# A curvature stage on five engines: one square per derivative, an identity product, and new orders

## The reference

```
g2 = ux * ux + uy * uy
denK = jnp.maximum(1.0 + g2, EPS)
K = jnp.clip((uxx * uyy - uxy * uxy) / (denK * denK + EPS), -5.0, 5.0)
denH = jnp.sqrt(1.0 + g2 + EPS)
H = ((1.0 + uy * uy) * uxx - 2.0 * ux * uy * uxy + (1.0 + ux * ux) * uyy) / (2.0 * denH ** 3 + EPS)
H = jnp.clip(H, -5.0, 5.0)
diff = jnp.clip(alpha * K + beta * H, -1.0, 1.0)
u = u + DT * diff
u = jnp.pad(u[:, :, 1:-1, 1:-1], ((0, 0), (0, 0), (1, 1), (1, 1)), mode='edge')
```

## Time and profile before

| | us |
|---|---|
| three runs | 699.22, 699.38, 702.49 (median 699.38) |
| profiled execution | 700.35 |
| its span | 698.5 |
| TensorE busy | 624.1 (89%) |
| VectorE busy | 389.5 (56%) |
| ScalarE busy | 314.6 (45%) |
| GpSimd busy | 253.5 (36%) |

### The profile page before, as it was taken

One profiled execution on the slowest core, in us unless ns is written; L12 is line 12 of the kernel. 1 busy time (PEld: TensorE's weight loads), 2 busy tenths in 40 slices (PEclk: granted clock), 3 DMA queues, 4 the chain that ended last, 5 costly groups with the idle time before them and its releaser, 6 DMA issues.

```text
span 698.5 us, 22687 instructions
## 1 busy us (share of the span) xinstructions
PE 624.1 (89%) x10128; PEld 362.1 (52%) x10128; DVE 389.5 (56%) x627; ACT 314.6 (45%) x582; POOL 253.5 (36%) x254
## 2 busy tenths in 40 slices
PE   5999699999996467778699879999999999999996
PEld 3785486466443233545355546555555555555551
DVE  4840000059213612223234427999999999999994
ACT  1300010043000001101122236999999999999993
POOL 1000000010001400000000006899999999999993
PEclk9999899999999766899999999999999999999999
DMA  9999999999999999999999544455455455455431
GB/s 367 433 420 381 426 432 425 427 429 421 430 424 422 431 426 428 428 429 424 429 424 423 187 120 128 116 132 136 126 132 135 128 131 136 127 131 138 125 84 61
DMA packets 33967, 201.69 MB, mean 289 GB/s; under 512 B 5504, under 2 KB 6928, under 8 KB 23632
## 3 DMA queue, kind: packets, MB, share of 16 engines
q1 hardware_dynamic: 33088, 198.53, 74.7%
q10 hardware_dynamic: 672, 1.41, 0.5%
q0 software_dynamic: 112, 0.32, 0.1%
HBM read 164.98 MB, written 1.84 MB: 239 GB/s over the span
## 4 chain that ended last, share of the span: by engine, by line
DVE 36%; PE 31%; DMA 26%; ACT 3%; issue 3%; SPq 0%; DVEq 0%; POOLq 0%; POOL 0%; ACTq 0%
DMA ring<-wout_w 16%; PE bank L407 8%; PE bank L423 7%; DVE ring L932 6%; DVE ring L935 6%; DVE ring L930 6%; PE bank L531 4%; PE bank L476 4%; DVE ring L928 4%; DMA ring<-wqk_p 3%; DVE ring L937 3%; DMA ring<-wv_w 3%; DMA ring<-wout_p 3%; DVE ring L956 3%; PE bank L557 3%
## 5 line engine op out<-in xcount | busy, mean ns | idle before, releaser
L597 PE MATMUL bank<-ring 32*32 32x480 f32 x5440 | 264.7, 570 | 2.6 <-DMA ring<-reg_a 2.6
L605 PE MATMUL bank<-ring 32*32 32x480 f32 x1600 | 177.3, 566 | 0.6 <-POOL ring L1148 0.6
L597 PEld LDWEIGHTS bank<-ring 32*32 32x32 f32 x5440 | 135.8, 103 | 70.9 <-issue 56.1
L1143 POOL TENSOR_TENSOR ring<-ring 128x480 f32<-128x480 f32 x40 | 48.9, 1223 | 178.5 <-DVE ring L935 178.5
L423 PE MATMUL bank<-ring,small 128*32 128x256 f32 x1152 | 81.6, 433 | 29.5 <-DMA ring<-wout_w 23.7
L423 PE MATMUL bank<-ring,xw 128*32 128x256 f32 x1024 | 61.8, 400 | 13.9 <-DMA ring<-wv_w 13.9
L423 PEld LDWEIGHTS bank<-ring,small 128*32 128x32 f32 x1152 | 40.0, 122 | 62.3 <-issue 30.0
L605 PEld LDWEIGHTS bank<-ring 32*32 32x32 f32 x1600 | 42.3, 104 | 56.9 <-issue 21.9
L407 PE MATMUL bank<-reg_a,ring 128*128 128x256 f32 x256 | 57.9, 388 | 3.4 <-DMA ring<-wqk_p 2.6
L767 DVE SCALAR_TENSOR_TENSOR reg_a<-bank,prm 128x512 f32<-128x512 f32 x4 | 2.8, 691 | 101.6 <-PE bank L483 101.6
L407 PEld LDWEIGHTS bank<-reg_a,ring 128*128 128x128 f32 x256 | 49.5, 195 | 11.6 <-DMA ring<-wqk_p 3.2
(11 more groups left out here) (181 smaller groups left out, 882.8 us busy)
## 6 DMA issues: line engine op xcount, KB each, us to landing
ring<-wv_w SPq DMA_DIRECT2D x32, 2048.0 KB, 28.4
ring<-wout_w SPq DMA_DIRECT2D x30, 2048.0 KB, 36.7
ring<-reg_a SPq DMA_DIRECT2D x60, 204.0 KB, 3.2
ring<-wqk_p SPq DMA_DIRECT2D x4, 2048.0 KB, 18.8
ring<-wqk_w SPq DMA_DIRECT2D x4, 2048.0 KB, 19.0
ring<-reg_a SPq DMA_DIRECT2D x60, 136.0 KB, 2.4
ring<-wv_p SPq DMA_DIRECT2D x2, 2048.0 KB, 18.9
ring<-wout_p SPq DMA_DIRECT2D x2, 2048.0 KB, 21.7
```

Source lines behind the costliest of these rows:

```text
L597: last = te.matmul(bank[QUAD * j:QUAD * (j + 1), field, 0:NF], mat(m, (j + t) % NCH), whole[at_, 2 + off:S + off, :], start=(n == 0), stop ...
L605: last = te.matmul(bank[at_, to, 0:NF], mat(m, j), from_[at_, :], start=start, stop=stop, skip_group_check=True)
L1143: p.tensor_tensor(cxy[now.q], f01[now.q][:, 0:NF], f01[now.q][:, NF:2 * NF], ALU.mult).then_inc(po["cxy"], 1)
```

## The change

Each first derivative is squared once. ScalarE squares uy into `p2`, as before, and ux straight into its bank (`sqr_x`); the bank's uy square is no longer ScalarE's work: TensorE multiplies `p2` by the identity into the bank of uy (`copy`), and outer waits for that. The arithmetic is otherwise the same.

All four engines get new orders inside the slot step, and some work changes its slot. In a step of TensorE, UYY and UXX are now those of now instead of old, the rest of UXY is that of old, and the first outer product is added at the end of the step for old. In a step of VectorE, clip2 and clip1 of now come first; then khk (old), the update and the edge copy (older), slope (now), khh (old), clipxy (now) and outer (now). ScalarE's new order is low (older), inverse of the first denominator (old), high (older), p2 and the x square (now), inverse of the second (old), the slope's logarithm, its square and its power 1.5, the square of uxy and the logarithm of both denominators (now). GpSimd's is the numerator of K (old), uxx·uyy and ux·uy (now), the two clips (old), cross (now). SP's program is not changed. A shortened diff:

```diff
 # TensorE
                 if old.live:
-                    te.wait_ge(ld_turn[2][old.c], 32 * (old.i + 1))
-                    if old.k > 1:
-                        te.wait_ge(ve["clip2"], old.k - 1)
-                    stencil(OUTER + 1, old, 3, UYY, 0)
-                    stencil(MIXED, old, 2, UXY, 2)
-                    ...
-                    stencil(OUTER, old, 1, UXX, 0)
-                    stencil(MIXED, old, 2, UXY, 3).then_inc(pe["fldxy"], 1)
-                if older.live:
-                    te.wait_ge(ve["outer"], older.k)
-                    add(bank_set(older.q) + 1, ONE, ab[older.q][:, 0:NF], True, False)
-                ...
+                    stencil(MIXED, old, 2, UXY, 1)
+                if now.live:
+                    te.wait_ge(ld_turn[2][now.c], 32 * (now.i + 1))
+                    if now.k > 1:
+                        te.wait_ge(ve["clip2"], now.k - 1)
+                    stencil(OUTER + 1, now, 3, UYY, 0)
                 if older.live:
                     add(bank_set(older.q) + 1, ONE, ab[older.q][:, NF:2 * NF], False, False)
+                if now.live:
+                    te.wait_ge(ld_turn[0][now.c], 32 * (now.i + 1))
+                    if now.k > 1:
+                        te.wait_ge(ve["clip2"], now.k - 1)
+                    stencil(OUTER, now, 1, UXX, 0)
                 if old.live:
+                    stencil(MIXED, old, 2, UXY, 2)
+                if now.live:
+                    stencil(OUTER + 1, now, 3, UYY, 1)
                 if older.live:
                     te.wait_ge(po["cross"], older.k)
                     add(bank_set(older.q) + 1, MINUS_TWO, cross[older.q], False, True).then_inc(pe["hn"], 1)
+                if now.live:
+                    stencil(OUTER, now, 1, UXX, 1)
                 if old.live:
+                    stencil(MIXED, old, 2, UXY, 3).then_inc(pe["fldxy"], 1)
+                if now.live:
+                    stencil(OUTER + 1, now, 3, UYY, 2)
+                    stencil(OUTER, now, 1, UXX, 2)
                 if old.live:
+                    te.wait_ge(ac["p2"], old.k)
+                    add(bank_set(old.q), ONE, p2[old.q], True, True).then_inc(pe["copy"], 1)
+                if now.live:
+                    stencil(OUTER + 1, now, 3, UYY, 3)
                     if now.k > 2:
                         te.wait_ge(ve["khk"], now.k - 2)
                     stencil(bank_set(now.q), now, 1, UY, 0)
+                    stencil(OUTER + 1, now, 3, UYY, 4).then_inc(pe["fld2"], 1)
+                    te.wait_ge(ld_turn[1][now.c], 32 * (now.i + 1))
+                    ...
+                    stencil(bank_set(now.q) + 1, now, 2, UX, 0)
                 ...
                     add(STEP, ALPHA, clip_k[older.q], True, False)
                 if now.live:
                     stencil(bank_set(now.q), now, 1, UY, 1)
                 ...
                     stencil(bank_set(now.q) + 1, now, 2, UX, 1)
                     stencil(bank_set(now.q), now, 1, UY, 2).then_inc(pe["fld1"], 1)
+                    if now.k > 1:
+                        te.wait_ge(ve["clipxy"], now.k - 1)
+                    stencil(MIXED, now, 2, UXY, 0)
+                if old.live:
+                    te.wait_ge(ve["outer"], old.k)
+                    add(bank_set(old.q) + 1, ONE, ab[old.q][:, 0:NF], True, False)
 # VectorE
+                if now.live:
+                    v.wait_ge(pe["fld2"], now.k)
+                    v.tensor_scalar(two(f34[now.q]), bank[:, OUTER:OUTER + 2, 0:NF], 10.0, -10.0, ALU.min, ALU.max).then_inc(ve["clip2"], 1)
                     v.wait_ge(pe["fld1"], now.k)
                     v.tensor_scalar(two(f01[now.q]), pair(now.q), 10.0, -10.0, ALU.min, ALU.max).then_inc(ve["clip1"], 1)
+                if old.live:
+                    ...
+                    v.tensor_tensor(kh[old.q][:, 0:NF], num[old.q], pair(old.q)[:, 0, :], ALU.mult).then_inc(ve["khk"], 1)
                 if older.live:
                     ...
+                if now.live:
+                    v.wait_ge(ac["p2"], now.k)
+                    v.wait_ge(ac["sqr_x"], now.k)
+                    v.scalar_tensor_tensor(slope[now.q], pair(now.q)[:, 1, :], 1.0, p2[now.q], ALU.add, ALU.add).then_inc(ve["slope"], 1)
                 if old.live:
                     ...
                     v.tensor_tensor(kh[old.q][:, NF:2 * NF], pair(old.q)[:, 1, :], inv_h[old.q], ALU.mult).then_inc(ve["khh"], 1)
+                if now.live:
+                    v.wait_ge(pe["fldxy"], now.k)
+                    v.tensor_scalar(mix[now.q], bank[:, MIXED, 0:NF], 10.0, -10.0, ALU.min, ALU.max).then_inc(ve["clipxy"], 1)
+                    v.wait_ge(ve["clip2"], now.k)
+                    v.wait_ge(pe["copy"], now.k)
+                    v.scalar_tensor_tensor(two(ab[now.q]), pair(now.q), 1.0, two(f34[now.q]), ALU.add, ALU.mult).then_inc(ve["outer"], 1)
# ScalarE
-                    a.activation(pair(old.q), f01[old.q].rearrange("p (x n) -> p x n", x=2), ACT.Square).then_inc(ac["sqr"], 1)
+                    a.activation(pair(now.q)[:, 1, :], f01[now.q][:, NF:2 * NF], ACT.Square).then_inc(ac["sqr_x"], 1)
```

More of the change, by code:

```diff
@@ L215, in build @@
             "slot_used", "patch_mean", "patch_var", "win_mean", "pool", "win_var", "pl_mean", "pl_var", "qkv",
-            "scores", "vt", "pt", "attn", "out", "ds", "conv", "fld1", "fld2", "fldxy", "step", "hn", "edge", "chunk")}
+            "scores", "vt", "pt", "attn", "out", "ds", "conv", "fld1", "fld2", "fldxy", "step", "hn", "edge", "chunk", "copy")}
         ve = {n: sem("ve_" + n) for n in (
@@ L655, in slot_step @@
                 if now.live:
[L656 to L660, removed]
                     stencil(bank_set(now.q), now, 1, UY, 1)
@@ L924, in slot_step @@
                 two = lambda a_: a_.rearrange("p (x n) -> p x n", x=2)
[L925 to L932, removed]
                 if now.live:
+                    v.wait_ge(pe["fld2"], now.k)
+                    v.tensor_scalar(two(f34[now.q]), bank[:, OUTER:OUTER + 2, 0:NF], 10.0, -10.0, ALU.min, ALU.max).then_inc(ve["clip2"], 1)
                     v.wait_ge(pe["fld1"], now.k)
                     v.tensor_scalar(two(f01[now.q]), pair(now.q), 10.0, -10.0, ALU.min, ALU.max).then_inc(ve["clip1"], 1)
-                    v.wait_ge(pe["fldxy"], now.k)
-                    v.tensor_scalar(mix[now.q], bank[:, MIXED, 0:NF], 10.0, -10.0, ALU.min, ALU.max).then_inc(ve["clipxy"], 1)
+                if old.live:
+                    v.wait_ge(po["num"], old.k)
+                    v.wait_ge(ac["invk"], old.k)
+                    v.tensor_tensor(kh[old.q][:, 0:NF], num[old.q], pair(old.q)[:, 0, :], ALU.mult).then_inc(ve["khk"], 1)
                 if older.live:
@@ L1077, in slot_step @@
                 if old.live:
[L1078 to L1080 removed]
+                    a.wait_ge(ve["outer"], old.k)
+                    a.wait_ge(ac["ln"], old.k)
+                    a.activation(pair(old.q)[:, 0, :], den[old.q][:, 0:NF], ACT.Exp, scale=-1.0).then_inc(ac["invk"], 1)
                 if older.live:
@@ L1086, in slot_step @@
                     a.activation(p2[now.q], f01[now.q][:, 0:NF], ACT.Square).then_inc(ac["p2"], 1)
+                    a.wait_ge(ve["clip1"], now.k)
+                    a.activation(pair(now.q)[:, 1, :], f01[now.q][:, NF:2 * NF], ACT.Square).then_inc(ac["sqr_x"], 1)
                 if old.live:
-                    a.wait_ge(ve["outer"], old.k)
-                    a.wait_ge(ac["ln"], old.k)
-                    a.activation(pair(old.q)[:, 0, :], den[old.q][:, 0:NF], ACT.Exp, scale=-1.0).then_inc(ac["invk"], 1)
                     a.wait_ge(ac["ln"], old.k)
                     a.activation(inv_h[old.q], den[old.q][:, NF:2 * NF], ACT.Exp, scale=-1.0).then_inc(ac["invh"], 1)
+                if now.live:
+                    a.wait_ge(ve["slope"], now.k)
+                    a.activation(lnw[now.q], slope[now.q], ACT.Ln, bias=D_EPS).then_inc(ac["lnw"], 1)
+                    a.wait_ge(ve["slope"], now.k)
+                    a.activation(den[now.q][:, 0:NF], slope[now.q], ACT.Square).then_inc(ac["psq"], 1)
+                    a.wait_ge(ac["lnw"], now.k)
+                    a.activation(den[now.q][:, NF:2 * NF], lnw[now.q], ACT.Exp, bias=LN2, scale=1.5).then_inc(ac["w15"], 1)
+                    a.wait_ge(ve["clipxy"], now.k)
+                    a.activation(sqm[now.q], mix[now.q], ACT.Square).then_inc(ac["sqxy"], 1)
+                    a.wait_ge(ac["psq"], now.k)
+                    a.wait_ge(ac["w15"], now.k)
+                    a.activation(den[now.q], den[now.q], ACT.Ln, bias=D_EPS).then_inc(ac["ln"], 1)
             a.wait_ge(po["padz"], 2)
@@ L1132, in slot_step @@
                 if old.live:
-                    p.wait_ge(ve["clipxy"], old.k)
-                    p.wait_ge(po["cxy"], old.k)
-                    p.tensor_tensor(cross[old.q], cxy[old.q], mix[old.q], ALU.mult).then_inc(po["cross"], 1)
-                    p.wait_ge(ve["clip2"], old.k)
```

(7 more changed lines are left out.)

36 lines of the change are left out of this document (5 added, 31 removed).

## The result

The changed kernel takes 747.47 us (median of four runs, 744.38 to 753.30), the kernel before in the same session 699.83. The ratio is 1.0678, 95% interval 1.0613 to 1.0743: 6.8% slower, 47.6 us. Predicted were 733 us, in a range of 717 to 755, and slower with a chance of 0.92. The direction, the mechanism and the range held; the likeliest value is 14 us short. The profiled execution took 744.38, its span 742.6.

The account below looks back on a forecast made before the run. The turn's landing plus UYY was taken as the bound: 443.4 us to clip2 of slot 4, 18 double steps of 14.9, tail 20.4 and 1.85 beyond the span give 733.9, predicted as 733 against the runs' median, range 717 to 755.

Parts of the forecast that it names:

- 2T >= 3.6 + 6.9 + 0.13 + 4.28: Two slot steps must fit first issue, turn's landing, semaphore and five UYY terms: 14.9 us, T = 7.45 where 6.57 stood.
- The start: First slots, before the turn bounds: clip2 of slot 1 at about 424.5 us, of slot 4 at 443.4.
- rival C: TensorE's clock falls to half: some 810 us, or 745 to 760 if only in a few steps; chance 0.06.
- The loop: Slots 4 to 40: 36 slots as 18 double steps of 14.9 us, 268.2 us, ending at 711.6.
- first issue, 3.6: From clip2, through update and edge copy, to SP's first transfer issue of the turn: 3.6 us.
- landing, 6.9: SP's six turn transfers, from first issue until all have landed: 6.9 us, ends 6.2 and 8.0.
- landing to clip2, 4.41: From the turn's landing to VectorE's clip2: semaphore 0.13 us, then five UYY terms and clip2's start 4.28.
- The semaphore to the first matmul: From the turn's landing to TensorE's first UYY product: 0.13 us.
- clearly other than 4.2: Sign of a wrong prediction: UYY's five terms on TensorE take clearly other than 4.2 us.
- The tail: From clip2 of slot 40 to the span's end: 20.4 us, 12.1 to khh and 8.3 after it.
- VectorE's floor: VectorE's nine instructions and edge copy alone: 3 x 1.07 + 5 x 0.57 + 0.09 + 0.12 = 6.27 us per step.
- rival A: The turn stays hidden and VectorE's 6.3 us step rules: 692.5 us, faster by 1.1%; chance 0.05.

Follow-up runs that it names:

- the first experiment: The changed kernel with later turn transfers reading and landing aside, so stencils keep the first turned image and wait for no later turn: 706.66 us, ratio 1.0078.
- the second: The changed kernel with SP issuing the transfers of shift 3 first, then 1, then 2: 713.16 us, ratio 1.0155.

## Why the prediction was right, and where it was short

**The mechanism: shown.** "2T >= 3.6 + 6.9 + 0.13 + 4.28": removing the wait gives 41 us back, landing the needed shift sooner 34, landing it later costs 35, and undoing the square's part changes nothing.

**The start** is right: clip2 of slot 1 was put at 424.5 and slot 4's at 443.4; they stand at 424.77 and 443.49.

**The clock** (rival C, 0.06) fell after all, but once in a while and not for the stage. In slot 37 TensorE stopped for 1.91 us, started again at 693.64, and its granted clock was 0.61 over the next stretch:

```profile
690.00:694.00 4.00, 2.09 (x48) 0.74 (x44) 3.29 (x6) 3.66 (x8) 3.27 (x4) 1.00 0.44 115
694.00:698.40 4.40, 4.40 (x101) 2.92 (x79) 1.22 (x2) 1.61 (x4) 1.08 (x2) 0.61 0.70 187
```

That slot's landing to clip2 is 6.34, 1.6 over. Stops of 2.19 and 1.82 in the same run, at 622 and 446, were not followed by it. I had argued from one stretch that kept its clock to none; the price was 0 to 3 us, well below the 12 to 27 that I gave for "a few steps".

**The loop** was put at 18 double steps of 14.9 and took 18 of 15.46, 10 us more. By its terms:

- first issue, 3.6: measured 3.75 on average. The update starts 2.80 after clip2 for 2.71, and the copy takes 0.25 on average for 0.17;
- landing, 6.9: measured 6.68 (5.69 to 7.87). The mean sixth issue is 3.44 after the first and the transfer 0.1 shorter;
- landing to clip2, 4.41: measured 4.74 in 26 of 36 slots. This is the mis-sized term. The semaphore to the first matmul takes 0.04, not 0.13 (0.11 by the two figures that it was worked out from), but UYY's ten passes on one set do not follow one another at 0.41 as in the earlier trace rows: the last starts 4.10 after the first, for 3.65. Between them stand the waits and products that the new order puts there. It is not the identity product: without it the term is 4.74 too, in 27 of 36 slots. Which of the others costs the 0.45 was not tried;
- the pairs: in nine of the other ten slots (the tenth is slot 37) the turn has landed in time, and TensorE, still at work on the step before, sets clip2, 6.52 after the last one; clip2 starts 0.04 after the last UYY product there too, as in all 36 slots. These ten bring the mean of the term to 5.04, and 3.75 + 6.68 + 5.04 = 15.47 is the double step. The forecast had no term for that: 2T was taken as if the turn were the limit in every slot.

The errors partly cancel: over 18 double steps the first issue adds 2.7 us and the last term 11.3, and the landing, 0.22 sooner, takes 4.0 back. The prediction had named "clearly other than 4.2" for UYY's five terms as a sign of being wrong. They take 4.66, where 4.23 was forecast; that moved the size, and the experiments show the mechanism all the same.

**The tail**, 20.4, is 20.9. With 1.8 beyond the span this is the profiled 744.38, and the runs' median lies 3 above that execution: its mean landing, 6.68, was the earliest of the four profiled.

**VectorE's floor** (rival A's 6.3) failed, though the forecast didn't hang on it. The edge copy was priced at 0.09 on the path from the earlier trace rows; once GpSimd works beside it, it takes 0.51. TensorE, counted at 5.7 us per slot, takes 6.52. Rival A would have ended at about 707 and not 692.5: even with the turn hidden there was nothing to gain. I had read a sum of starts as a floor without asking who runs beside each instruction in the new order.

## What to carry to other kernels

A new order is to be priced by its longest chain across steps, and transfers that show no wait can come onto that chain when their reader moves one step earlier: write down for each how many steps lie between issue and use, before and after. When a reader moves, move the issue order with it; one line gave back 34 of 48 us here. A time saved on an engine counts only up to the next chain, and two experiments show where that was: the ring of slope, inverse and khk at 6.47 us a step in the old orders, and TensorE at 6.52 in the new ones, where 6.57 stood before.

## What the runs showed of the hardware

VectorE's copy of 128x32 takes 0.17 to 0.18 us where GpSimd is idle at its start (35 of the 36 copies of before). Where a product of GpSimd is running, the copy ends 0.03 to 0.06 after the product does, whenever it started (36 copies each of after, of the first experiment and of the second): it took 0.18 to 0.20 when it began 1.05 to 1.09 into the product, 0.31 to 0.34 at 0.91 to 0.93, 0.57 to 0.62 at 0.64 to 0.67, and 0.84 to 0.86 at 0.41. The copy of the kernel after that is shown above, 568.77 + 0.33 = 569.10, had this product of GpSimd beside it, which ends at 569.06:

```profile
567.86 1.20 POOL L1146 TENSOR_TENSOR ring<-ring 128x480 f32<-128x480 f32 x1
```

VectorE's other instructions keep their length beside GpSimd's products. The Trainium skill (SBUF — State Buffer, section "Who interferes with whom") says that VectorE's copies, in some modes, and GpSimd's instructions take a shared pair of ports that one holds for its whole instruction while the other waits; these ends agree with that.

SP issues a transfer in 0.6 us, but in 21 of the 204 issues between 434 and 700 us it took over 0.7, up to 2.06 (29 of 216 and 2.35 before); the cause isn't in the trace.
